# Second graph layer on one core: reordered pair pipeline, and two result tiles finished by ScalarE and GpSimd

## What is computed

```python
h = relu(layernorm(x));  x = x + L0(h, adj)      # first layer
h = relu(layernorm(x));  x = x + L1(h, adj)      # second layer, the one around the change

def L1(h, b, edge):                  # b and edge are both adj
    mask = graph_id[:, None] == graph_id[None, :]          # 32 graphs of 64 nodes
    query = h @ Wq.T + bq;  key = h @ Wk.T + bk;  value = h @ Wv.T + bv
    a = where(mask, query @ key.T * scale, 0.0)
    scores = (a + b + edge) * where(mask, 1.0, -1e6)
    return (softmax(scores) * mask) @ value
```

## Time and profile before

| | |
|---|---|
| median of 3 runs | 241.07 us (240.69 to 242.31) |
| the profiled execution's own time | 242.53 us |
| its span, first to last instruction | 240.7 us |
| TensorE busy in the span | 226.2 us, 94% |
| VectorE / ScalarE / GpSimd busy | 187.1 / 158.8 / 61.6 us |

### The profile page before, as it was taken

The page is one execution under the profiler, slowest core; times in us unless marked ns, Lnnn a source line. Parts: engine busy times, 40 slices in busy tenths (PEclk is TensorE's granted clock), DMA queues, the critical chain, the costliest instruction groups (busy, mean ns, idle before and its releaser), DMA issues.

```text
span 240.7 us, 5432 instructions
## 1 busy us (share of the span) xinstructions
PE 226.2 (94%) x2072; PEld 197.0 (82%) x2072; DVE 187.1 (78%) x454; ACT 158.8 (66%) x303; POOL 61.6 (26%) x117
## 2 busy tenths in 40 slices
PE   7889999999999999999999999999999999769972
PEld 7778887888887888888888888888888889659960
DVE  2799888699775777499984499987699587778694
ACT  3778817897555847695661794767995646759750
POOL 2633770000006000001820001820021224356550
PEclk9999999999799999999999999999999999999999
DMA  6999498019797000454310000000000000011214
GB/s 185 312 391 373 108 394 297 3 32 346 203 396 249 1 3 0 157 206 163 124 53 3 1 3 1 4 0 0 3 0 3 0 0 4 3 45 44 67 45 157
DMA packets 20091, 26.34 MB, mean 109 GB/s; under 512 B 1888, under 2 KB 11872, under 8 KB 20064
## 3 DMA queue, kind: packets, MB, share of 16 engines
q1 hardware_dynamic: 19520, 25.72, 31.0%
q10 hardware_dynamic: 544, 0.27, 0.4%
HBM read 23.88 MB, written 2.10 MB: 108 GB/s over the span
## 4 chain that ended last, share of the span: by engine, by line
PE 76%; DVE 11%; ACT 3%; issue 3%; DMA 2%; POOL 2%; SPq 1%; DVEq 0%; ACTq 0%; POOLq 0%
PE bank_b L1030 23%; PE bank_a L1054 12%; PE bank_a L1056 11%; PE bank_a L1058 11%; PE bank_a L978 7%; PE bank_l L978 3%; DMA adjt<-in_x 2%; PE bank_b L978 2%; PE bank_a L1192 1%; PE bank_l L970 1%; DVE adjt L1788 1%; PE bank_l L1080 1%; POOL st L594 1%; DVE adjt L1800 1%; PE bank_l L1103 1%
## 5 line engine op out<-in xcount | busy, mean ns | idle before, releaser
L1056 PE MATMUL bank_a<-hd,e_hi 128*128 128x257 f16 x256 | 70.7, 276 | 0.0
L1054 PE MATMUL bank_a<-hd,e_hi 128*128 128x257 f16 x256 | 70.1, 274 | 0.0
L1058 PE MATMUL bank_a<-hd,e_lo 128*128 128x257 f16 x256 | 70.0, 273 | 0.0
L1030 PE MATMUL bank_b<-hb,adjt 128*128 128x259 f16 (+1 forms) x512 | 67.2, 275 | 0.2 <-DVE xb L1589 0.2
L1030 PEld LDWEIGHTS bank_b<-hb,adjt 128*128 128x128 bf16 x512 | 49.8, 98 | 7.8 <-DVE xb L1589 0.5
L695 ACT ACTIVATE e_hi<-e_slot 128x1024 f16<-128x1024 f32 x32 | 33.7, 1052 | 29.5 <-PE bank_a L1058 18.5
L1603 DVE SCALAR_TENSOR_TENSOR e_lo<-e_slot,e_hi 128x1024 f16<-128x1024 f32 x32 | 39.0, 1219 | 9.5 <-ACT e_hi L695 9.4
L1597 DVE SCALAR_TENSOR_TENSOR e_slot<-e_slot,adjt 128x1024 f32<-128x1024 f32 x32 | 39.0, 1218 | 9.1 <-ACT e_slot L688 9.0
L688 ACT ACTIVATE e_slot<-s_row,nbias 128x512 f32<-128x512 f32 x64 | 42.3, 710 | 0.2
L564 POOL TENSOR_TENSOR rs_all<-veb,half_neg 128x2 f32<-128x2 f32 x8 | 6.6, 819 | 90.1 <-DVE veb L1770 90.1
L1058 PEld LDWEIGHTS bank_a<-hd,e_lo 128*128 128x128 f16 x256 | 25.3, 99 | 3.5
(11 more groups left out here) (238 smaller groups left out, 387.9 us busy)
## 6 DMA issues: line engine op xcount, KB each, us to landing
adjt<-in_adj_t SPq DMA_DIRECT2D x16, 1024.0 KB, 8.6
x_all<-in_x SPq DMA_DIRECT2D x4, 512.0 KB, 5.2
out<-adjt SPq DMA_DIRECT2D x16, 128.0 KB, 1.8
adjt<-in_x SPq DMA_DIRECT2D x3, 512.0 KB, 6.5
diag<-in_adj SPq DMA_DIRECT2D x16, 64.0 KB, 3.5
adjt<-in_x SPq DMA_DIRECT2D x2, 256.0 KB, 3.6
e_slot<-in_L_gnn_W_gcnb ACTq DMA_DIRECT2D x1, 256.0 KB, 3.8
e_slot<-in_W_saT SPq DMA_DIRECT2D x1, 256.0 KB, 4.7
```

Source lines behind the costliest of these rows:

```text
L1030: eng.matmul(B[:, r % 2, 0:cols], adjt_block(k, j, r), hb16[:, j, part, 0:cols], start=(j == 0 and part == 0), stop=(j == NT - 1 and part ...
L1054: eng.matmul(A[:, r, 0:D + 1], high, hd16[:, j, 0, 0:D + 1], start=(j == 0), stop=False, skip_group_check=True)
L1056: eng.matmul(A[:, r, 0:D + 1], high, hd16[:, j, 1, 0:D + 1], start=False, stop=False, skip_group_check=True)
L1058: mm = eng.matmul(A[:, r, 0:D + 1], low, hd16[:, j, 0, 0:D + 1], start=False, stop=(j == NT - 1), skip_group_check=True)
```

## The change

All engines' orders in the second layer are rewritten from the same point on.

- **Middle, VectorE.** mix(LAST, 2) and mix(LAST, 3) come ahead of h1T_low(3), maxima and keep_values(2). add_mix(LAST, 2, 4) is cut into add_only (right behind h1T_low(4)) and new_moments (the sums, behind maxima(2)). The loop runs for p = 4 to 6; shifts for tiles 12, 13 comes ahead of it, that for 14, 15 behind keep_values(4). The row bias of pair 0 is made by VectorE.
- **Middle, ScalarE.** tanh_mix(LAST, 2, 4) and h1T_high(4) come ahead of the first exponents; values_high(2) behind pT_high(0).
- **Middle, GpSimd.** row_bias(0) is dropped. A wait for x1_ready = 16 stands ahead of values_low(2). The last inv_new_deviation is ahead of row_sums(1).
- **End.** TensorE has turn_p(4), scores(6), keys(7), values(7, 0), turn_p(5), gather(4), values(7, 1), scores(7), and turn_last(1) ahead of gather(6). VectorE drops last_values_high; ScalarE does values_high(7). results(5) and results(6) write their first tile only. GpSimd's values_low(7) is behind outer_part(7).
- **Second tiles of pairs 5 and 6** (output tiles 11 and 13): ScalarE scales from PSUM (scale_second), GpSimd adds x1, ScalarE's queue issues the two stores.
- **Semaphores.** iota_made is counted in consts_made, gates_squared in w4_squared, with the waits renumbered.

```diff
@@ sync
+                eng.wait_ge(o_ready, i + 1 - (i > NT - 5) - (i > NT - 3))
-            for i in range(NT): store(i)
+            for i in range(NT):
+                if i not in (NT - 5, NT - 3):
+                    store(i)
@@ gpsimd
-            row_bias(0)
             outer_part(0)
             row_bias(1)
             outer_part(1)
+            eng.wait_ge(x1_ready, NT)
             values_low(2)
             row_sums(0)
             for p in range(4, NQ - 1):
                 row_bias(p - 2)
                 outer_part(p - 2)
                 values_low(p - 1)
-                row_sums(p - 3)
                 if p == 4:
                     inv_new_deviation(CT * LAST + 2, NT)
+                row_sums(p - 3)
...
             outer_part(NQ - 2)
-            values_low(NQ - 1)
             row_sums(NQ - 2)
             outer_part(NQ - 1)
+            values_low(NQ - 1)
             row_sums(NQ - 1)
+            for p in (NQ - 3, NQ - 2):
+                i = 2 * p + 1
+                eng.wait_ge(o_scaled, p - (NQ - 4))
+                eng.tensor_tensor(o_sb[:, p, 1, :], o_sb[:, p, 1, :], x1_all[:, i * D:(i + 1) * D], ALU.add) \
+                   .then_inc(o_added, 1)
@@ scalar
-            values_high(2)
+            tanh_mix(LAST, 2, CT)
+            h1T_high(4)
             exponents(0, 0)
             exponents(0, 1)
-            tanh_mix(LAST, 2, CT)
-            for p in range(3, NQ - 1):
-                if p > 3:
-                    values_high(p - 1)
+            keys_high(3)
+            pT_high(0)
+            values_high(2)
+            exponents(1, 0)
+            exponents(1, 1)
+            for p in range(4, NQ - 1):
+                values_high(p - 1)
...
             exponents(NQ - 3, 0)
-            keys_high(NQ - 1)
             pT_high(NQ - 4)
             exponents(NQ - 3, 1)
+            keys_high(NQ - 1)
+            pT_high(NQ - 3)
             exponents(NQ - 2, 0)
             exponents(NQ - 2, 1)
-            pT_high(NQ - 3)
+            values_high(NQ - 1)
             exponents(NQ - 1, 0)
...
+            def scale_second(p):
+                eng.wait_ge(rz_ready, p + 1)
+                eng.wait_ge(pv_summed, p + 1)
+                eng.wait_ge(o_ready, 2 * (NQ - 3) + p - (NQ - 4))
+                i = 2 * p + 1
+                eng.activation(o_sb[:, p, 1, :], result_bank(p)[:, D:2 * D], ACT.Copy, scale=rz[:, i:i + 1]) \
+                   .then_inc(o_scaled, 1)
+            def store_second(p):
+                eng.wait_ge(o_added, p - (NQ - 4))
+                i = 2 * p + 1
+                eng.dma_start(out[i * P:(i + 1) * P, :], o_sb[:, p, 1, :]).then_inc(o_stored, 16)
+            scale_second(NQ - 3)
+            scale_second(NQ - 2)
+            store_second(NQ - 3)
+            store_second(NQ - 2)
@@ tensor
+            turn_p(NQ - 4)
+            scores(NQ - 2)
             keys(NQ - 1)
-            turn_p(NQ - 4)
             values(NQ - 1, 0)
-            scores(NQ - 2)
+            turn_p(NQ - 3)
+            gather(NQ - 4)
             values(NQ - 1, 1)
-            turn_p(NQ - 3)
             scores(NQ - 1)
-            gather(NQ - 4)
             turn_p(NQ - 2)
             gather(NQ - 3)
             turn_last(0)
+            turn_last(1)
             gather(NQ - 2)
-            turn_last(1)
@@ vector
-                for n in range(2):
+                for n in range(1 if p in (NQ - 3, NQ - 2) else 2):
...
             keys_low(2)
-            keep_values(2)
+            mix(LAST, 2)
+            mix(LAST, 3)
+            shifts(NT - 4, NT - 2)
             h1T_low(3)
             maxima(0)
+            keep_values(2)
             maxima(1)
-            mix(LAST, 2)
-            mix(LAST, 3)
-            for p in range(3, NQ - 1):
-                if p >= 4:
+            h1T_low(4)
+            add_only(LAST, 2, CT)
+            keys_low(3)
+            pT_low(0)
+            keep_values(3)
+            maxima(2)
+            new_moments(LAST, 2, CT)
+            for p in range(4, NQ - 1):
+                if p > 4:
                     maxima(p - 2)
-                    results(p - 4)
+                results(p - 4)
                 h1T_low(p + 1)
                 keys_low(p)
-                if p in (3, 4):
-                    shifts(2 * p + 6, 2 * p + 8)
                 pT_low(p - 3)
                 keep_values(p)
-                if p == 3:
-                    add_mix(LAST, 2, CT)
+                if p == 4:
+                    shifts(NT - 2, NT)
             maxima(NQ - 3)
             results(NQ - 5)
-            keys_low(NQ - 1)
             pT_low(NQ - 4)
             maxima(NQ - 2)
-            keep_values(NQ - 1)
-            last_values_high()
-            maxima(NQ - 1)
+            keys_low(NQ - 1)
             pT_low(NQ - 3)
             results(NQ - 4)
+            keep_values(NQ - 1)
+            maxima(NQ - 1)
+            results(NQ - 3)
             pT_low(NQ - 2)
-            results(NQ - 3)
             pT_low_last(0)
             pT_low_last(1)
             results(NQ - 2)
```

## The result

| | before | after |
|---|---|---|
| median (20 runs each) | 243.38 us | 239.15 us |
| all runs | 240.69 to 244.51 | 236.77 to 241.67 |
| profiled execution: time, span | 242.53, 240.7 | 239.23, 237.3 |
| start of turn_h1(3), the last point that both share | 199.92 | 200.29 |
| from there to the end of the span ("the stage" below) | 40.78 | 37.01 |

A forecast was written before the change was run, and what follows sets the result against it. TensorE's 4.84 us a pair was taken as the bound after 199.8 us, broken by waits for pT_low. Gains of 1.80 + 2.29 + 0.66 = 4.75 us take the median from 241.07 to 236.3; range 235.3 to 239.0.

The forecast's parts named there:

- What bounds the kernel: Second layer's per-pair pipeline after 199.8 us: TensorE sets the time at 4.84 us a pair where that period holds.
- In three places: TensorE's period breaks ahead of gather(0), gather(1) and gather(5), idle 1.58, 2.22 and 0.98 us, each waiting for pT_low.
- The first gap: TensorE's idle ahead of gather(0): the start moves from 208.30 to 206.50, 1.80 us gained.
- the second gap: TensorE's idle ahead of gather(1): it starts 4.09 us earlier than 215.54, so 2.29 us more gained.
- Rival B: Half of the middle's gain stays away through delays in ScalarE's and GpSimd's orders: 238.6 or nearer 240; chance 0.16.
- The end: From gather(3) to VectorE's last end: 11.50 us instead of 12.39, 0.89 less; 0.66 gained after the added second tiles.
- That is 0.23 behind results_last: GpSimd's second addition, taken as 0.68 us, ends 0.23 us after VectorE's results_last, cutting the end's gain to 0.66.
- In the tail a store of 128 KB from SP lands in 1.8 us ... I take 1.8: The last store, now from ScalarE's queue, was taken to land in 1.8 us like SP's stores, leaving the sum unchanged.
- Rival A: Tail: the store from ScalarE's queue lands 2.0 us later, time 238.3; chance 0.10.
- Rival C: VectorE instructions with two SBUF inputs lock with GpSimd's values_low, up to 1.16 us each, 242.1 to 244.4; in full 0.04.
- Rival D: TensorE's clock at 0.50 among dense products costs 0.75 us, time 237.1; chance 0.08 together with one VectorE-GpSimd lock.
- I take differences from the span and apply them to the median: Base of the forecast: the gain, from the profiled span of 240.70, is taken off the runs' median of 241.07 us.

The follow-up runs named there:

- end_undone: The changed kernel with every engine's end taken from the kernel before, so only the middle is changed; stage 36.69 us, ratio 0.986 to the kernel before.
- before_late_values_low: The kernel before with only GpSimd's values_low(7) moved behind outer_part(7); stage 40.1 us against 40.78, ratio 0.998.

## Why the prediction was right and wrong

- **"What bounds the kernel": right.** Nothing changed ahead of turn_h1(3), and TensorE's 4.84 us a pair is the pace after (4.84 and 4.85). "In three places" was not complete: the kernel before also waits 0.38 us ahead of gather(6) and 0.24 ahead of the last pair's first product. Both waits are gone after, and the forecast's walk from gather(3) to VectorE's end had them in its total.
- **"The first gap", "the second gap", 1.80 + 2.29: right to 0.02.** This execution's turn_h1(3) is 0.37 later than in the profile of before. With it, gather(0), (1), (2), (3) were forecast at 206.87, 211.82, 216.67 and 221.52, and came at 206.87, 211.81, 216.66 and 221.50. end_undone alone gives the 4.09. The walk rested on the steps between starts of an engine's instructions, 0.08 us shorter than their recorded durations. Rival B, with spare times of 0.04 to 0.15 us at four places, did not occur at any.
- **"The end", VectorE: 0.89 forecast, 0.82 measured** (12.39 less 11.57 from gather(3) to VectorE's end). The idle ahead of gather(5) is 0.65 (0.74), the row bias 0.22 (0.22), gather(6) on the point.
- **"That is 0.23 behind results_last": a term mis-sized; it measured 0.41.** The addition took 0.72, between its bounds of 0.20 and 1.16 and near the 0.68 taken. The rest is the second scaling: it starts 0.12 after the end of the tile of results(6) that it waits for by the code (its bracket names L1876, the last pair's row scale, for which it has no wait), and the addition 0.08 after its end, where the walk had 0.03.
- **"In the tail a store of 128 KB from SP lands in 1.8 us ... I take 1.8": failed, 0.75 us.** Rival A had the place right (the store from ScalarE's queue) and the reason wrong: no queue is slower. SP's own fetch of instructions comes in among the last stores and holds back nine packets, as many as one DMA engine's share. The forecast counted which stores each queue issues, not that two stores less and the new order bring SP to the fetch at another moment. 0.82 - 0.41 - 0.75 = -0.34, the end's value as measured (-0.32 by end_undone).
- **Rival C did not occur**: no new VectorE instruction of 128x2 met a values_low. Its mechanism is real, as before_late_values_low shows, and 0.66 us of what VectorE gained at the end is the end of such a meeting. **Rival D**: the stretch at 0.50 is in both kernels and is not the change's.
- **"I take differences from the span and apply them to the median": failed, the larger part.** The profiled execution (242.53) had the stretch at half clock in the earlier trace rows and two of the three runs (240.69, 241.07) lay, by their times, on the level without it (their clocks aren't on record), so the base was that level's and not the kernel's. 243.38 - 4.75 is 238.6, inside the range; with the stage as measured, 243.38 - 3.77 = 239.6, for 239.15 measured. Of the 2.85 us between 236.3 and 239.15 the base makes 2.31 (243.38 - 241.07). The warning was on the page: the profiled execution stood 1.5 us above the median. The range took in every unknown of the change and nothing for the base, though the three runs alone spread over 1.6 us.

## What to carry to other kernels

Where an order is written by hand, walk it from the last common point with steps between starts, not with recorded durations; that gave four landmarks to 0.02 us here. Look in the DMA view for instruction transfers among the last stores before moving work for a few tenths of a microsecond: 0.7 us hung on them, and 20 instructions on SP that do no work won it back. And when the profiled execution is off the median of few runs, if only by 0.6% as here (242.53 against 241.07), say which clock level each stands on, and put the distance between the levels into the range.

## What the runs showed of the hardware

- A block of instructions that is fetched among the last stores holds back nine packets of 144: the last store lands in 2.5 to 2.8 us (eight profiles) instead of 1.8 to 1.9 (the three with SP padded, the same stores otherwise).
- The granted clock of one program falls to half in some executions and not in others: for 3 us behind 20 one-column float32 products (10 of 17 profiles), and near the start (7 of 20). The level medians lie 2.7 us apart after and 3.0 before, more than most edits here give.
- GpSimd's addition of 128x256 float32 takes 0.72 to 0.73; an issue of a 128 KB store takes SP 0.33 to 0.5.
